# First routing stage: x laid out by partitions, tiles moved in pairs, router logits made with tokens on the partitions

## The chip, the cores and the metric

The kernel runs on one NeuronCore of a Trainium2 chip. The metric is the device time in microseconds (us) of one execution. An execution is made of one program that holds all stages of a two-layer network one behind the other; engines meet at a barrier between stages.

Engines are called PE (TensorE; PE for its matmuls, PEld for the loads of its stationary operand), DVE (VectorE), ACT (ScalarE), POOL (GpSimd) and SP (SyncE, which here only issues DMAs). A suffix q (SPq) means the engine's sequencer.

## What is computed

Activations are x, 2 x 2048 tokens by 512 features in fp32. The reference runs, in this order: a mixture-of-experts block, attention, the mixture block again, a gated feed-forward block, a second kind of attention, and the feed-forward block again. The change is in the first mixture block, whose routing part is:

```python
m = jnp.mean(x, axis=-1, keepdims=True); v = jnp.var(x, axis=-1, keepdims=True)
y = (x - m) / jnp.sqrt(v + 1e-5)                      # layer norm; y is the experts' input
var = jnp.mean(jnp.square(y), axis=-1, keepdims=True)
router_input = y * rsqrt(var + 1e-6) * 512 ** -0.5 * router_scale
logits = einsum('gsd,de->gse', router_input, router_logits)    # 8 experts
probs = softmax(logits); choices = top 2 of logits
# each token goes to its 2 experts, weighted by the renormalised probabilities
```

From the choices follows a plan: the pairs (token, expert) sorted by expert, cut into tiles of 128 slots, with the row of y that belongs into each slot.

## The kernel before

The 4096 tokens are 32 tiles of 128 tokens (NT = 32). In tile t, partition p holds token 128 t + p. `experts(0, x[0])` calls `routing_stage` and then `expert_stage`. The first routing (`given` is None) makes layer norm, the router's logits and the plan; the second routing gets its logits from `output_stage` (`given`) and only makes the plan, so that its tile loop does not exist.

The tile loop of the first routing, by engine:

- SP (L190 to L217) loads four tiles ahead (NX = 4, `load`, L193: 256 KB, 2 KB for each partition), then the router's weights `wl`, `rs` and the experts' scale `esc` on the same queue. For each tile it waits for y of that tile (L204), issues the load of the tile four later into the freed buffer, and the store of y to `yn` in DRAM (L207). After the loop it issues twelve loads of 512 KB with expert weights (L213).
- DVE (L345 on) first makes `wr`, the router's weights times the router's scale (L358), which waits for all three small loads. Then for each tile: `bn_stats` of the next tile (L362), reciprocal of the deviation (L378), `bn_aggr` of the next tile (L365), y itself (L384) and a copy of the variance (L369). y of tile t waits for the store that last used its buffer and for yT of tile t - 4.
- PE (L291 on): `turn` (L293) transposes a tile of y into PSUM with four matmuls against the identity (L297). `step` (L300) makes the logits of tile t with four fp32 matmuls, each of which the profile shows as two instructions (L304), and then turns tile t + 2. PE's order is thus turn 0, turn 1, logits 0, turn 2, logits 1, turn 3 and so on; its queue is served in this order. In the logits `wr` (128 x 8) is the stationary operand and the 128 columns of yT stream by, so the result has experts on the partitions: 8 x 128.
- ACT (L257 on): the deviation of the next tile (L261), yT from PSUM to SBUF (L267), and `keep` (L271), which copies the 8 x 128 logits of the tile before into `lgT` (L273).

Behind the loop PE turns the 32 pieces of `lgT` back to tokens on the partitions (L317 to L320, 32 transposes of 8 x 128), and DVE multiplies them with `rr`, the inverse of the root mean square (L408). DVE then picks the two best experts and makes the plan (L412 to L488). Meanwhile ACT and POOL prepare the weights of the first expert (L283 to L289, L253). `expert_stage` begins when all are done: its POOL gathers rows of `yn` by the plan (L536).

Two later places read or write what the change lays out anew: `projection_stage` loads tiles of x again (L860), and `output_stage` stores the y of the second mixture block to `yn` (L1514).

Of the kernel before, what the change touches and what calls it, by code (L numbers as in the profile page):

```python
# [15 lines left out]
ALU = mybir.AluOpType  # L16
# [3 lines left out]
P = 128  # L20
B, S, D = 2, 2048, 512
# [96 lines left out]
def routing_stage(nc, stage, const, x, scale, logits_w, expert_scale, w_experts, box, yn, plan, given=None):  # L118


    with ExitStack() as ctx:
        mem = Memory(nc, ctx, stage)
        NX = 4
        xb = mem.sb("xb", [P, NX, D])
        yb = mem.sb("yb", [P, NX, D])
# [40 lines left out]
        tr = mem.ps("tr", [P, 2, D])  # L166
        lg_ps = mem.ps("lg", [P, NT, E])
        pre_ps = mem.ps("pre", [P, E, NT])
# [3 lines left out]

        lgT_ps = [t[0:E].rearrange("e t f -> e (t f)")[:, 0:P] for t in (pre_ps, tot_ps)]
        tot_cols, count_ps = tot_ps[:, 0, 0:E // EH], tot_ps[:, 1, 0:E]

        x_in, y_st, raw_in = mem.sems("x_in", NX), mem.sems("y_st", NX), mem.sems("raw_in", WPIECES)
        whi_rdy, neg_rdy, wlo_in, next_in = mem.sem("whi_rdy"), mem.sem("neg_rdy"), mem.sems("wlo_in", 2), mem.sem("next_in")
        HOT = 8
        w_in, wr_rdy, iotas, ones_set, picked = (mem.sem(n) for n in ("w_in", "wr_rdy", "iotas", "ones_set", "picked"))
        bn_rdy, mv_rdy, sd_rdy, rstd_rdy, y_rdy, tr_rdy, yT_rdy, lgT_rdy, lgT_kept, lg_rdy = (  # L180
            mem.sem(n) for n in ("bn_rdy", "mv_rdy", "sd_rdy", "rstd_rdy", "y_rdy", "tr_rdy", "yT_rdy", "lgT_rdy", "lgT_kept", "lg_rdy"))
# [3 lines left out]
        block = ctx.enter_context(nc.Block())  # L185

        def piece(buf, n):
            return buf[:, n * WPIECE:(n + 1) * WPIECE]

        @block.sync  # L190
        def _(sp):
            def load(t, k):
                sp.dma_start(xb[:, k, :], x[bass.ds(t * P, P), :]).then_inc(x_in[k], 16)  # L193

            if not given:
                for t in range(NX):
                    load(t, t)
                    sp.sem_inc(y_st[t], 16)
                sp.dma_start(wl[:], logits_w).then_inc(w_in, 16)
                sp.dma_start(rs[:], scale).then_inc(w_in, 16)  # L200
            sp.dma_start(esc[:], expert_scale.partition_broadcast(P)).then_inc(w_in, 16)

            def step(t, k, i, last):
                sp.wait_ge(y_rdy, t + 1)  # L204
                if not last:
                    load(t + NX, k)
                sp.dma_start(yn[bass.ds(t * P, P), :], yb[:, k, :]).then_inc(y_st[k], 16)  # L207

            if not given:
                looped(sp, NT, NX, step)  # L210
            for n in range(2 * WPIECES):
                arrived = raw_in[n] if n < WPIECES else next_in
                sp.dma_start(piece(box["lo"], n).bitcast(F32), w_experts[n // WPIECES, :, n % WPIECES, :]).then_inc(arrived, 16)  # L213
            if not given:
                for k in range(NX):
                    sp.wait_ge(y_st[k], 16 * (NT // NX + 1))
            sp.wait_ge(next_in, 16 * WPIECES)  # L217

        @block.gpsimd
        def _(pool):  # L220
# [3 lines left out]
            pool.iota(iota_row[:], [[1, P]], base=0, channel_multiplier=0, allow_small_or_imprecise_dtypes=True).then_inc(iotas, 1)  # L224
            pool.iota(token[:], [[0, TOPK], [P, NT]], base=0, channel_multiplier=1, allow_small_or_imprecise_dtypes=True).then_inc(iotas, 1)
            pool.iota(number[:], [[0, 1]], base=0, channel_multiplier=1, allow_small_or_imprecise_dtypes=True).then_inc(iotas, 1)
# [30 lines left out]
        @block.scalar  # L257
        def _(act):
            def deviation(t, k):
                act.wait_ge(mv_rdy, t + 1)  # L260
                act.activation(sd[:, bass.ds(t, 1)], mv[:, k % 2, 1:2], ACT.Sqrt, bias=const["eps"][:]).then_inc(sd_rdy, 1)  # L261

            def step(t, k, i, last):
                if not (last and k == NX - 1):
                    deviation(t + 1, k + 1)
                act.wait_ge(tr_rdy, t + 1)
                act.activation(yT[:, k % 2, :], tr[:, k % 2, :], ACT.Copy).then_inc(yT_rdy, 1)  # L267
                if not (isinstance(t, int) and t == 0):
                    keep(t - 1, (k - 1) % 2)

            def keep(t, k):  # L271
                act.wait_ge(lgT_rdy, t + 1)
                act.activation(lgT[0:E, bass.ds(t, 1), :], lgT_ps[k].unsqueeze(1), ACT.Copy).then_inc(lgT_kept, 1)  # L273

            if not given:
                deviation(0, 0)
                looped(act, NT, NX, step, head=True)
                keep(NT - 1, (NT - 1) % 2)
                act.wait_ge(step_done, 3)
                act.activation(small["msd"][:], small["ms"][:], ACT.Sqrt).then_inc(msd_rdy, 1)  # L280
            act.wait_ge(gap_rdy, 1)
            act.activation(small["egap"][:], small["gap"][:], ACT.Exp).then_inc(egap_rdy, 1)
            for n in range(WPIECES):  # L283
                act.wait_ge(raw_in[n], 16)
                act.activation(piece(box["hi"], n), piece(box["lo"], n).bitcast(F32), ACT.Copy).then_inc(whi_rdy, 1)
                if n >= 2:
                    act.wait_ge(wlo_in[n % 2], 16 * (n // 2))
                act.wait_ge(whi_rdy, n + 1)
                act.activation(box["raw"][:, n % 2, :], piece(box["hi"], n).bitcast(F32), ACT.Copy, scale=-1.0).then_inc(neg_rdy, 1)  # L289

        @block.tensor  # L291
        def _(pe):
# [7 lines left out]
            def step(t, k, i, last):  # L300
                pe.wait_ge(yT_rdy, t + 5)
                pe.wait_ge(lgT_kept, t + 1)
                for c in range(DC):
                    ins = pe.matmul(lgT_ps[k % 2], wr[:, c, :], yT[:, k % 2, c * P:(c + 1) * P],  # L304
                                    start=(c == 0), stop=(c == DC - 1), skip_group_check=True)
                ins.then_inc(lgT_rdy, 1)
                if not (last and k >= NX - 2):
                    turn(t + 2, k + 2)

            if not given:  # L310
                pe.sem_inc(yT_rdy, 4)
                pe.sem_inc(lgT_kept, 2)
                pe.wait_ge(wr_rdy, DC)
                turn(0, 0)
                turn(1, 1)
                looped(pe, NT, NX, step)
                pe.wait_ge(lgT_kept, NT + 2)  # L317
                for t in range(NT):
                    ins = pe.transpose(lg_ps[:, t, :], lgT[0:E, t, :], const["ident"][0:E, 0:E])
                ins.then_inc(lg_rdy, 1)  # L320
            pe.wait_ge(both_rdy, 1)
# [24 lines left out]
        def _(dve):  # L346
            steps = [0]

            def then(ins):

                steps[0] += 1
                ins.then_inc(step_done, 1)
                dve.wait_ge(step_done, steps[0])
# [6 lines left out]
            def stats(t, k, i):  # L360
                dve.wait_ge(x_in[k], 16 * (i + 1))
                dve.bn_stats(bn[:, k % 2, :], xb[:, k, :]).then_inc(bn_rdy, 1)  # L362
# [8 lines left out]
            def step(t, k, i, last):  # L371
# [9 lines left out]
                dve.wait_ge(rstd_rdy, t + 1)  # L381
                dve.wait_ge(y_st[k], 16 * (i + 1))
                dve.wait_ge(yT_rdy, t + 1)
# [9 lines left out]
            else:  # L393
# [10 lines left out]
                then(dve.reciprocal(small["rr"][:], small["msd"][:]))  # L404
                dve.wait_ge(lg_rdy, 1)
                dve.wait_ge(iotas, 2)
                lg = wide["lg"]
                then(dve.tensor_tensor(lg[:], lg_ps[:], spread(small["rr"][:], E), ALU.mult))  # L408

# [412 lines left out]
def projection_stage(nc, stage, const, x, x_new, joined, q_w, k_w, v_w, q_parts, kst, v, spare):  # L822

    with ExitStack() as ctx:
# [33 lines left out]
        def _(sp):  # L858
            def load(t):
                sp.dma_start(xb[:, t % NX, :], x[bass.ds(t * P, P), :]).then_inc(x_in[t % NX], 16)  # L860

# [617 lines left out]
def output_stage(nc, stage, const, attn, w_hi, w_lo, x, x_new, scale, logits_w, yn, logits_out):  # L1479

    with ExitStack() as ctx:
# [26 lines left out]
        def _(sp):  # L1508
# [1021 lines left out]
def layout(np, i):  # L2530

    def chunked(w):
        return w.reshape(w.shape[0] // P, P, -1).transpose(1, 0, 2)
# [4 lines left out]
    def column(v):  # L2538
# [40 lines left out]
```

## Time and profile before

| | us |
|---|---|
| median of 3 runs | 4752.76 (4750.65 to 4758.85) |
| profiled execution, its own time | 4751.44 |
| span of the profiled execution | 4749.9 |
| first routing stage, to DVE's last instruction | 0 to 114.7 |
| expert stage 0, from PE's first instruction | 115.7 |

The page of the profile gives busy times of the engines over the whole span; for one stage the timeline, the windows and the waits are asked with a stretch in us from the start of the span. "PEclk" or "granted clock" is the share of TensorE's full clock: 1.00 is 2.4 GHz and 0.50 is 1.2 GHz. A timeline row is: start, duration, engine, line, operation, output<-inputs, shapes, count, and in brackets the idle time before it with what ended it. Several instructions that follow each other are one row with a count, and its duration is from the first start to the last end.

### The profile page before, as it was taken

To read this page: it belongs to the slowest core of one execution; us is meant where nothing else is said; L and a number is where in the kernel's file an instruction comes from. 1 tells how busy PE (TensorE), PEld (TensorE's weight loads), DVE (VectorE), ACT (ScalarE), POOL (GpSimd) and SP (SyncE) were. 2 spreads that over 40 slices of the span, in tenths; PEclk is the share of its full clock that TensorE was granted. 3 is DMA by queue.
4 is the path that set the end of the run, shared out by engine and by line. 5 is a ranking of instruction groups with operands and counts; after the bars stand their busy time and mean duration, and the time that the engine had idled before them with its cause. 6 is when DMAs were issued, how large, how long until landed. Compare 5 with 4: busy or idle time off the path is not lost. (4 is left out here: it accounts for less than half of the span.)

```text
span 4749.9 us, 81453 instructions
## 1 busy us (share of the span) xinstructions
PE 4566.0 (96%) x27934; PEld 3496.3 (74%) x27935; DVE 2873.2 (60%) x5253; ACT 2101.9 (44%) x4079; POOL 2252.9 (47%) x1724
## 2 busy tenths in 40 slices
PE   6999996899999999999999799999899999999999
PEld 4888885666666666666666688888788877778888
DVE  7222225789999999999984533323455548754444
ACT  4222224466676767676764322222333235433322
POOL 0545433278888888888882154643111007500000
PEclk8999998899999999999999799999899999999999
DMA  7232326757777777777765633433422112250110
GB/s 222 89 103 93 105 78 230 247 105 147 146 145 146 146 151 148 146 147 146 147 140 161 192 97 126 138 118 109 176 67 71 54 51 82 75 196 27 36 36 27
DMA packets 241401, 577.68 MB, mean 122 GB/s; under 512 B 30304, under 2 KB 84576, under 8 KB 216544
## 3 DMA queue, kind: packets, MB, share of 16 engines
q0 software_dynamic: 62064, 317.23, 29.7%
q1 hardware_dynamic: 178928, 255.47, 16.3%
q8 instruction: 198, 3.24, 0.3%
q14 instruction: 211, 1.73, 0.1%
HBM read 254.88 MB, written 121.63 MB: 79 GB/s over the span
## 5 line engine op out<-in xcount | busy, mean ns | idle before, releaser
L1410 POOL TENSOR_TENSOR attend_pairs<-attend_pt 128x1024 f32<-128x1024 f32 x512 | 1258.5, 2476 | 197.8 <-ACT attend_pt L1375 197.6
L1423 DVE TENSOR_REDUCE attend_mx<-attend_am_ps 128x1 f32<-128x512 f32 x2048 | 1251.4, 678 | 126.4 <-PE attend_am_ps L1283 123.0
L1375 ACT ACTIVATE attend_pt<-attend_sc_ps 128x512 f32<-128x512 f32 x2048 | 1040.2, 617 | 284.5 <-PE attend_sc_ps L1271 284.4
L1283 PE MATMUL attend_am_ps<-attention_kst,attend_qst 96*128 96x512 f32 x2048 | 859.9, 425 | 10.8 <-DMA attend_qst<-q_parts 10.7
L1271 PE MATMUL attend_sc_ps<-attend_qst,attention_kst 98*128 98x512 f32 x2048 | 816.9, 400 | 1.5 <-ACT attend_pt L1375 1.3
L1283 PEld LDWEIGHTS attend_am_ps<-attention_kst,attend_qst 96*128 96x128 f32 x2048 | 393.2, 192 | 241.4 <-DVE attend_mx L1423 123.1
L1775 PE MATMUL ffn_gu_ps<-ffn_y_hi,ffn_w 128*128 128x512 f32 (+1 forms) x1584 | 567.0, 367 | 3.1 <-DVE ffn_y_lo L1905 3.0
L1775 PE MATMUL ffn_gu_ps<-ffn_y_lo,ffn_w 128*128 128x512 f32 (+1 forms) x1584 | 566.3, 367 | 0.0
L768 DVE TENSOR_TENSOR expert_ac<-expert_gu_ps,expert_gl 128x512 f32<-128x512 f32 x142 | 98.2, 691 | 748.1 <-ACT expert_gl L715 748.1
L1297 PE MATMUL attend_pv_ps<-attend_pt,attention_v 128*32 128x256 f32 x8192 | 493.6, 381 | 0.0
L1271 PEld LDWEIGHTS attend_sc_ps<-attend_qst,attention_kst 98*128 98x128 f32 x2048 | 389.8, 191 | 87.7 <-ACT attend_pt L1375 11.7
L1297 PEld LDWEIGHTS attend_pv_ps<-attend_pt,attention_v 128*32 128x32 f32 x8192 | 246.2, 110 | 211.8 <-ACT attend_pt L1375 46.4
L1847 ACT ACTIVATE ffn_sg<-ffn_gu_ps,ffn_gs 128x512 f32<-128x512 f32 (+1 forms) x198 | 127.4, 644 | 568.4 <-PE ffn_gu_ps L1775 568.2
L715 ACT ACTIVATE expert_gl<-expert_gu_ps 128x512 f32<-128x512 f32 x142 | 85.0, 599 | 628.9 <-PE expert_gu_ps L645 628.9
L645 PE MATMUL expert_gu_ps<-weights_hi,expert_x_hi 128*128 x1088 | 342.5, 396 | 4.6 <-issue 1.8
L1775 PEld LDWEIGHTS ffn_gu_ps<-ffn_y_hi,ffn_w 128*128 128x128 f32 x1584 | 300.6, 190 | 52.5 <-DVE ffn_y_lo L1905 3.6
L1775 PEld LDWEIGHTS ffn_gu_ps<-ffn_y_lo,ffn_w 128*128 128x128 f32 x1584 | 300.7, 190 | 48.1
L645 PE MATMUL expert_gu_ps<-weights_lo,expert_x_hi 128*128 x1088 | 335.9, 390 | 0.0
L645 PE MATMUL expert_gu_ps<-weights_hi,expert_x_lo 128*128 x1088 | 335.4, 389 | 0.0
L1915 DVE SCALAR_TENSOR_TENSOR ffn_hf<-ffn_gu_ps,ffn_us,ffn_sg 128x512 f32<-128x512 f32 (+1 forms) x198 | 136.9, 691 | 318.9 <-PE ffn_gu_ps L1775 311.1
L1791 PE MATMUL ffn_dn_ps<-ffn_w,ffn_h_hi 128*128 128x512 f32 x704 | 276.6, 393 | 0.0
L1791 PE MATMUL ffn_dn_ps<-ffn_w,ffn_h_lo 128*128 128x512 f32 x704 | 274.2, 390 | 0.0
(350 smaller groups left out, 7461.6 us busy)
## 6 DMA issues: line engine op xcount, KB each, us to landing
attend_pairs<-attend_pairs POOLq DMA_DIRECT2D x189, 1024.0 KB, 7.4
weights_raw<-experts_dram POOLq DMA_DIRECT2D x76, 512.0 KB, 4.1
ys<-expert_ob SPq DMA_DIRECT2D x142, 256.0 KB, 2.0
attend_qst<-q_parts SPq DMA_DIRECT2D x192, 128.0 KB, 3.9
ffn_xb<-x SPq DMA_DIRECT2D x64, 256.0 KB, 2.9
keyvalue_xb<-x SPq DMA_DIRECT2D x64, 256.0 KB, 2.8
weights_lo<-experts_dram SPq DMA_DIRECT2D x24, 512.0 KB, 8.9
ffn_w<-ffn_kept SPq DMA_DIRECT2D x22, 512.0 KB, 9.2
```

The source lines that it names most:

```text
L645: ins = pe.matmul(gu[:, q, :], a, w[:, bass.ds(off + (c * WPIECE + q * H), H)], start=(c == 0 and n == 0), stop=(c == DC - 1 and n == 2))
L768: dve.tensor_tensor(ac[:, k, :], gu[:, 1, :], gl[:, k, :], ALU.mult).then_inc(ac_rdy, 1)
L1271: pe.matmul(sc[:, s % SBANKS, :], kst[0:KROWS + 2, o:o + P], qst[0:KROWS + 2, n % 2, hh:hh + 4, :], start=True, stop=True).then_inc(s_rdy, 1)
L1283: pe.matmul(am[:, bank, :], qst[0:KROWS, n % 2, h * HALF + hd, :], kst[0:KROWS, o:o + 4 * P], start=True, stop=True).then_inc(am_rdy, 1)
L1297: ins = pe.matmul(pv[HD * j:HD * (j + 1), 0, :], v[:, (n // QT) * QT + kt, :], pt[:, u % RING, 2 * P * j:2 * P * (j + 1)], start=(kt == 0) ...
L1375: act.activation(pt[:, u % RING, g * 4 * P:(g + 1) * 4 * P], sc[:, s % SBANKS, :], ACT.Exp, scale=HD ** -0.5).then_inc(p_rdy, 1)
L1410: pool.tensor_tensor(pairs[:, slot(half, j), :], pt[:, 2 * p % RING, :], pt[:, (2 * p + 1) % RING, :], ALU.add).then_inc(pair_rdy, 1)
L1423: dve.tensor_reduce(mx[:, hh, block:block + 1], am[:, am_slot["max", a] % MBANKS, :], AX.X, ALU.max).then_inc(mx_rdy, 1)
L1775: ins = pe.matmul(gu[:, k, q, 0:width], a, b, start=(c == 0 and n == 0), stop=(c == DC - 1 and n == 1))
L1791: ins = pe.matmul(dn[:, j % 2, :], a, b, start=(m == 0 and n == 0), stop=(m == IC - 1 and n == 1))
L1847: act.activation(sg[:, k, 0:n], gu[:, k, 0, 0:n], ACT.Silu, scale=gs[:, m:m + 1]).then_inc(sg_rdy, 1)
L1915: dve.scalar_tensor_tensor(hf[:, k, 0:n], gu[:, k, 1, 0:n], us[:, m:m + 1], sg[:, k, 0:n], ALU.mult, ALU.mult).then_inc(h_rdy, 1)
```

## The change

In the first routing x comes from the host laid out as 128 partitions x 32 tiles x 512 (`chunked`), so that two neighbouring tiles are 4 KB in a row for each partition, 64 KB from one partition to the next. Tiles are loaded and y is stored in pairs of 512 KB, with eight tiles (four pairs) in flight; the eight load buffers lie in the space of `lgT`, which no longer holds logits. `yn` gets the same order: token (tile t, partition p) is row 32 p + t; `token` in the plan follows, and so do the store in `output_stage` and the load in `projection_stage`, which stay single tiles. In the logits the operands swap: yT (128 x 128) is the stationary operand and the 8 columns of `wr` stream by, so that the result is 128 tokens x 8 and `keep` copies it straight to `lg`. The 32 transposes behind the loop go. The loop is unrolled eight times instead of four.

```diff
-        NX = 4
-        xb = mem.sb("xb", [P, NX, D])
+        NX = 8
...
+        xb = lgT[:].rearrange("p (n a) b -> p n (a b)", n=NX)
...
-        lgT_ps = [t[0:E].rearrange("e t f -> e (t f)")[:, 0:P] for t in (pre_ps, tot_ps)]
+        lg_ps = [t[:, 0:1, 0:E] for t in (pre_ps, tot_ps)]
...
-            def load(t, k):
-                sp.dma_start(xb[:, k, :], x[bass.ds(t * P, P), :]).then_inc(x_in[k], 16)
+            def load(pair, k):
+                sp.dma_start(xb[:, 2 * k:2 * k + 2, :], x[:, bass.ds(pair * 2, 2), :]).then_inc(x_in[k], 16)
...
-            def step(t, k, i, last):
-                sp.wait_ge(y_rdy, t + 1)
+            def step(pair, k, i, last):
+                sp.wait_ge(y_rdy, pair * 2 + 2)
                 if not last:
-                    load(t + NX, k)
-                sp.dma_start(yn[bass.ds(t * P, P), :], yb[:, k, :]).then_inc(y_st[k], 16)
+                    load(pair + NX // 2, k)
+                sp.dma_start(y_rows[:, bass.ds(pair * 2, 2), :], yb[:, 2 * k:2 * k + 2, :]).then_inc(y_st[k], 16)
...
-            pool.iota(token[:], [[0, TOPK], [P, NT]], base=0, channel_multiplier=1, ...)
+            pool.iota(token[:], [[0, TOPK], [1, NT]], base=0, channel_multiplier=NT, ...)
...
             def keep(t, k):
-                act.wait_ge(lgT_rdy, t + 1)
-                act.activation(lgT[0:E, bass.ds(t, 1), :], lgT_ps[k].unsqueeze(1), ACT.Copy).then_inc(lgT_kept, 1)
+                act.wait_ge(lg_rdy, t + 1)
+                act.activation(wide["lg"][:, bass.ds(t, 1), :], lg_ps[k], ACT.Copy).then_inc(lg_kept, 1)
...
                 for c in range(DC):
-                    ins = pe.matmul(lgT_ps[k % 2], wr[:, c, :], yT[:, k % 2, c * P:(c + 1) * P],
+                    ins = pe.matmul(lg_ps[k % 2], yT[:, k % 2, c * P:(c + 1) * P], wr[:, c, :],
                                     start=(c == 0), stop=(c == DC - 1), skip_group_check=True)
...
                 looped(pe, NT, NX, step)
-                pe.wait_ge(lgT_kept, NT + 2)
-                for t in range(NT):
-                    ins = pe.transpose(lg_ps[:, t, :], lgT[0:E, t, :], const["ident"][0:E, 0:E])
-                ins.then_inc(lg_rdy, 1)
...
-                dve.wait_ge(lg_rdy, 1)
+                dve.wait_ge(lg_kept, NT + 2)
                 lg = wide["lg"]
-                then(dve.tensor_tensor(lg[:], lg_ps[:], spread(small["rr"][:], E), ALU.mult))
+                then(dve.tensor_tensor(lg[:], lg[:], spread(small["rr"][:], E), ALU.mult))
...
# projection_stage
-                sp.dma_start(xb[:, t % NX, :], x[bass.ds(t * P, P), :]).then_inc(x_in[t % NX], 16)
+                sp.dma_start(xb[:, t % NX, :], x[:, t, :]).then_inc(x_in[t % NX], 16)
...
# output_stage
-                sp.dma_start(yn[t * P:(t + 1) * P, :], yb[:, t % NX, :]).then_inc(y_st[t % NX], 16)
+                sp.dma_start(yn.rearrange("(p t) d -> p t d", t=NT)[:, t, :], yb[:, t % NX, :]).then_inc(y_st[t % NX], 16)
...
-        "x": i["L0_attn_x"].reshape(T, D),
+        "x": chunked(i["L0_attn_x"].reshape(T, D)),
```

## Rows read from the trace of the kernel before

**Rows 1.** The page, busy us with share of the span and instructions.

```profile
PE 4566.0 (96%) x27934; PEld 3496.3 (74%) x27935; DVE 2873.2 (60%) x5253; ACT 2101.9 (44%) x4079; POOL 2252.9 (47%) x1724
```

**Rows 2.** Windows: stretch, length, busy us of five engines, PEclk, DMA share, GB/s.

```profile
4.00:8.00 4.00, 0.00 (x0) 0.00 (x0) 0.00 (x0) 0.46 (x1) 2.31 (x34) 1.00 0.88 269
20.00:40.00 20.00, 17.03 (x128) 11.18 (x128) 15.68 (x54) 11.51 (x33) 0.00 (x0) 1.00 0.89 274
40.00:60.00 20.00, 16.89 (x128) 10.98 (x125) 15.45 (x54) 11.85 (x33) 0.00 (x0) 1.00 0.91 275
78.00:82.00 4.00, 0.00 (x0) 0.00 (x0) 3.73 (x10) 0.00 (x0) 0.00 (x0) 0.53 1.03 421
```

**Rows 3.** Waits of DVE, 0 to 110 us: total us, times, longest.

```profile
DVE route_wr L358 <- DMA route_esc<-expert_scale_dram: 9.0, 1, 9.0
DVE route_bn L362 <- DMA route_xb<-x_dram: 6.3, 11, 0.9
```

**Rows 4.** Timeline of DVE, y of tiles 0, 29 and 31.

```profile
11.87 0.55 DVE L384 TENSOR_SCALAR route_yb<-route_xb,route_mv,route_rstd 128x512 f32<-128x512 f32 x1
...
67.13 0.55 DVE L384 TENSOR_SCALAR route_yb<-route_xb,route_mv,route_rstd 128x512 f32<-128x512 f32 x1
...
70.19 0.55 DVE L384 TENSOR_SCALAR route_yb<-route_xb,route_mv,route_rstd 128x512 f32<-128x512 f32 x1
```

**Rows 5.** Timeline of PE, first tiles of the loop.

```profile
12.52 1.09 PE L297 MATMUL route_tr_ps<-all_ident,route_yb 128*128 128x128 f32 x4 [12.52 <-DVE route_yb L384]
14.01 1.12 PE L297 MATMUL route_tr_ps<-all_ident,route_yb 128*128 128x128 f32 x4 [0.40 <-DVE route_yb L384]
15.06 1.88 PE L304 MATMUL route_pre_ps<-route_yT,route_wr 128*8 128x128 f32 x8
16.86 0.66 PE L297 MATMUL route_tr_ps<-all_ident,route_yb 128*128 128x128 f32 x4
17.45 1.04 PE L304 MATMUL route_tot_ps<-route_yT,route_wr 128*8 128x128 f32 x8
```

**Rows 6.** Timeline of PE, the last tiles of the output stage.

```profile
2662.36 0.95 PE L1644 MATMUL output_lg_ps<-output_wr,output_yT 128*128 128x8 f32 x8
...
2664.49 1.06 PE L1644 MATMUL output_lg_ps<-output_wr,output_yT 128*128 128x8 f32 x8 [0.69 <-ACT output_yT L1544]
2665.41 1.80 PE L1636 MATMUL output_tr_ps<-all_ident,output_yb 128*128 128x128 f32 x8
2667.05 3.58 PE L1644 MATMUL output_lg_ps<-output_wr,output_yT 128*128 128x8 f32 x16
```

**Rows 7.** Windows in the plan and in the output stage, columns as in rows 2.

```profile
96.00:114.00 18.00, 14.99 (x68) 14.07 (x66) 17.90 (x30) 4.69 (x5) 2.58 (x3) 0.50 0.59 117
2650.00:2662.00 12.00, 12.00 (x73) 10.45 (x72) 7.03 (x17) 3.95 (x8) 0.00 (x0) 1.00 0.39 146
2666.00:2670.00 4.00, 4.00 (x20) 3.77 (x19) 0.52 (x2) 1.31 (x3) 0.00 (x0) 0.50 0.18 67
```

**Rows 8.** Timeline of the routing's loop end, from the last logits on.

```profile
72.42 1.04 PE L304 MATMUL route_tot_ps<-route_yT,route_wr 128*8 128x128 f32 x8
...
73.49 0.27 ACT L273 ACTIVATE route_lgT<-route_tot_ps 8x128 f32<-8x128 f32 x1 [0.61 <-PE route_tot_ps L304]
...
73.81 2.14 PE L319 MATMUL route_lg_ps<-all_ident,route_lgT 8*128 8x8 f32 x32 [0.36 <-ACT route_lgT L273]
...
73.98 0.35 DVE L404 RECIPROCAL route_rr<-route_msd 128x32 f32<-128x32 f32 x1 [2.70 <-ACT route_msd L280]
76.04 0.42 DVE L408 TENSOR_TENSOR route_lg<-route_lg_ps,route_rr 128x256 f32<-128x256 f32 x1 [1.71 <-PE route_lg_ps L319]
```

**Rows 9.** Timeline: POOL's last weight add and DVE's last instruction of the stage.

```profile
103.07 0.86 POOL L253 DMA_DIRECT2D weights_lo<-weights_raw  x1 [1.76 <-ACT weights_raw L289]
...
114.48 0.23 DVE L488 CAST weights_rows<-route_rows_ps 128x72 uint32<-128x72 f32 x1 [0.33 <-PE route_rows_ps L342]
```

**Rows 10.** Windows, inside the projection stage, columns as in rows 2.

```profile
820.00:880.00 60.00, 58.31 (x288) 46.76 (x287) 57.21 (x122) 34.38 (x68) 24.57 (x26) 1.00 1.02 369
```

More of the change, by code:

```diff
@@ L166, in routing_stage @@
         tr = mem.ps("tr", [P, 2, D])
-        lg_ps = mem.ps("lg", [P, NT, E])
         pre_ps = mem.ps("pre", [P, E, NT])
@@ L171, in routing_stage @@
         tab_ps = mem.ps("tab", [1, 5, SLOT_TILES])
-        lgT_ps = [t[0:E].rearrange("e t f -> e (t f)")[:, 0:P] for t in (pre_ps, tot_ps)]
+        lg_ps = [t[:, 0:1, 0:E] for t in (pre_ps, tot_ps)]
         tot_cols, count_ps = tot_ps[:, 0, 0:E // EH], tot_ps[:, 1, 0:E]
-        x_in, y_st, raw_in = mem.sems("x_in", NX), mem.sems("y_st", NX), mem.sems("raw_in", WPIECES)
+        x_in, y_st, raw_in = mem.sems("x_in", NX // 2), mem.sems("y_st", NX // 2), mem.sems("raw_in", WPIECES)
         whi_rdy, neg_rdy, wlo_in, next_in = mem.sem("whi_rdy"), mem.sem("neg_rdy"), mem.sems("wlo_in", 2), mem.sem("next_in")
@@ L179, in routing_stage @@
         w_in, wr_rdy, iotas, ones_set, picked = (mem.sem(n) for n in ("w_in", "wr_rdy", "iotas", "ones_set", "picked"))
-        bn_rdy, mv_rdy, sd_rdy, rstd_rdy, y_rdy, tr_rdy, yT_rdy, lgT_rdy, lgT_kept, lg_rdy = (
-            mem.sem(n) for n in ("bn_rdy", "mv_rdy", "sd_rdy", "rstd_rdy", "y_rdy", "tr_rdy", "yT_rdy", "lgT_rdy", "lgT_kept", "lg_rdy"))
+        bn_rdy, mv_rdy, sd_rdy, rstd_rdy, y_rdy, tr_rdy, yT_rdy, lg_rdy, lg_kept = (
+            mem.sem(n) for n in ("bn_rdy", "mv_rdy", "sd_rdy", "rstd_rdy", "y_rdy", "tr_rdy", "yT_rdy", "lg_rdy", "lg_kept"))
         step_done, msd_rdy, gap_rdy, egap_rdy, both_rdy, summed, totals_rdy, ranked, tile_rdy, token_rdy, row_rdy, rows_rdy, tab_rdy, turned = (
@@ L185, in routing_stage @@
         block = ctx.enter_context(nc.Block())
+        y_rows = yn.rearrange("(p t) d -> p t d", t=NT)
         def piece(buf, n):
@@ L191, in _ @@
         def _(sp):
-            def load(t, k):
-                sp.dma_start(xb[:, k, :], x[bass.ds(t * P, P), :]).then_inc(x_in[k], 16)
+            def load(pair, k):
+                sp.dma_start(xb[:, 2 * k:2 * k + 2, :], x[:, bass.ds(pair * 2, 2), :]).then_inc(x_in[k], 16)
             if not given:
-                for t in range(NX):
-                    load(t, t)
-                    sp.sem_inc(y_st[t], 16)
+                for pair in range(NX // 2):
+                    load(pair, pair)
+                    sp.sem_inc(y_st[pair], 16)
                 sp.dma_start(wl[:], logits_w).then_inc(w_in, 16)
@@ L201, in _ @@
             sp.dma_start(esc[:], expert_scale.partition_broadcast(P)).then_inc(w_in, 16)
-            def step(t, k, i, last):
-                sp.wait_ge(y_rdy, t + 1)
+            def step(pair, k, i, last):
+                sp.wait_ge(y_rdy, pair * 2 + 2)
                 if not last:
-                    load(t + NX, k)
-                sp.dma_start(yn[bass.ds(t * P, P), :], yb[:, k, :]).then_inc(y_st[k], 16)
+                    load(pair + NX // 2, k)
+                sp.dma_start(y_rows[:, bass.ds(pair * 2, 2), :], yb[:, 2 * k:2 * k + 2, :]).then_inc(y_st[k], 16)
             if not given:
-                looped(sp, NT, NX, step)
+                looped(sp, NT // 2, NX // 2, step)
             for n in range(2 * WPIECES):
@@ L214, in _ @@
             if not given:
-                for k in range(NX):
+                for k in range(NX // 2):
                     sp.wait_ge(y_st[k], 16 * (NT // NX + 1))
@@ L224, in _ @@
             pool.iota(iota_row[:], [[1, P]], base=0, channel_multiplier=0, allow_small_or_imprecise_dtypes=True).then_inc(iotas, 1)
-            pool.iota(token[:], [[0, TOPK], [P, NT]], base=0, channel_multiplier=1, allow_small_or_imprecise_dtypes=True).then_inc(iotas, 1)
+            pool.iota(token[:], [[0, TOPK], [1, NT]], base=0, channel_multiplier=NT, allow_small_or_imprecise_dtypes=True).then_inc(iotas, 1)
             pool.iota(number[:], [[0, 1]], base=0, channel_multiplier=1, allow_small_or_imprecise_dtypes=True).then_inc(iotas, 1)
@@ L301, in step @@
                 pe.wait_ge(yT_rdy, t + 5)
-                pe.wait_ge(lgT_kept, t + 1)
+                pe.wait_ge(lg_kept, t + 1)
                 for c in range(DC):
-                    ins = pe.matmul(lgT_ps[k % 2], wr[:, c, :], yT[:, k % 2, c * P:(c + 1) * P],
+                    ins = pe.matmul(lg_ps[k % 2], yT[:, k % 2, c * P:(c + 1) * P], wr[:, c, :],
                                     start=(c == 0), stop=(c == DC - 1), skip_group_check=True)
-                ins.then_inc(lgT_rdy, 1)
+                ins.then_inc(lg_rdy, 1)
                 if not (last and k >= NX - 2):
@@ L311, in _ @@
                 pe.sem_inc(yT_rdy, 4)
-                pe.sem_inc(lgT_kept, 2)
+                pe.sem_inc(lg_kept, 2)
                 pe.wait_ge(wr_rdy, DC)
@@ L360, in stats @@
             def stats(t, k, i):
-                dve.wait_ge(x_in[k], 16 * (i + 1))
+                dve.wait_ge(x_in[k // 2], 16 * (i + 1))
                 dve.bn_stats(bn[:, k % 2, :], xb[:, k, :]).then_inc(bn_rdy, 1)
@@ L381, in step @@
                 dve.wait_ge(rstd_rdy, t + 1)
-                dve.wait_ge(y_st[k], 16 * (i + 1))
+                if k % 2 == 0:
+                    dve.wait_ge(y_st[k // 2], 16 * (i + 1))
                 dve.wait_ge(yT_rdy, t + 1)
```

## Prediction

> **What bounds the kernel now.** I read the page first: PE is busy for 96% of the span, but that is an average over stages, and the change touches one of 115 us [rows 1]. So I ask that stage: windows, waits, timeline. In the tile loop no engine is full: in 20 us PE is busy for 17.0, DVE for 15.7, and the DMA engines are 0.89 to 0.91 busy at 274 GB/s [rows 2]. DVE's waits say what is late: 6.3 us for tiles of x, and 9.0 us for the small loads ahead of the loop [rows 3]. y of tile 0 starts at 11.87 and of tile 31 at 70.19, 1.88 us a tile; undisturbed tiles (29 to 31) take 3.06 / 2 = 1.53 us [rows 4]. So the loop is bound by DMA on top of a DVE that is nearly as slow, and PE, with 0.59 us of transposes and about 1 us of logits a tile [rows 5], is close behind. All three matter: whichever gets slower sets the end.
>
> After the loop a serial chain of DVE ends the stage at 114.7; ACT's and POOL's weight work issues its last add at 103.07 [rows 9] and has 7 us to spare after some 4.5 of landing, so it follows any shift of the loop unseen. Each microsecond of the loop is one of the kernel, since the stages behind start at a barrier.
>
> **The start.** The first four loads carry 2.1 MB instead of 1.05 MB, and the small loads wait behind them. Between 4 and 8 us 1.08 MB came at 269 GB/s; loads with 4 KB for each partition (expert weights) run at 421 GB/s [rows 2]. At that rate 2.1 MB take 5.0 us instead of 4: +1.0 us for `wr` and so for y 0 (12.9). Bounds: 0, if the small loads slip through, and +3.8, if 4 KB gain nothing (1.05 MB at 275). I take 1.0, because the weight loads have the same packet size.
>
> **DMA in the loop.** A tile moves 524 KB in and out: 1.9 us at 275 GB/s, 1.25 us at 421 [rows 2]. Loads at the new size leave the path; what pairs add in waiting (y leaves after every second tile, the first load after two) is hidden by six more tiles in flight. By this alone DVE would set about 1.55 us a tile.
>
> **PE in the loop, the step that decides.** Per tile PE keeps four transposes and eight logits instructions, but each logits instruction now loads 128 x 128 and streams 8 columns, where it loaded 128 x 8 and streamed 128. The output stage does just this operation (L1644): eight in 0.95 us at full clock [rows 6]. At full clock nothing is lost.
>
> Will the clock be at 2.4 GHz? The loop before starts slow: four transposes take 1.09 us at 12.52, 0.66 at 16.86 [rows 5]. So PE ran at the lower level until some 3 us of transposes and of logits that stream 128 columns were behind it (the windows print 1.00 there, since no change was recorded before; the durations tell). In the output stage PE has 1.00 while 512-column products fill it. When these end, at 2662.4, and only transposes and new-form logits are left, PE goes on in 2664.49 and 2665.41 and the clock falls in the middle of it; from 2666 to 2670 PE is busy for 4.00 of 4.00 us with transposes and these logits, the same mix as the new loop, and the clock stays at 0.50 [rows 6, 7]. The plan agrees: 64 matmuls with a full weight load and 72 columns keep PE busy for 15 of 18 us, at 0.50 throughout [rows 7]. I conclude that in this mix being busy does not bring the clock. The new loop begins at 1.2 GHz, as the old one did, and from its third group has nothing but this mix: it stays at 1.2 GHz to its end.
>
> The Trainium skill ("TensorE: Matmul & The Clock Gate", "HAM oscillation — how this bites in real kernels") speaks against that: it asks only that PE has no idle gaps. PE has none in the new loop, so by the page the clock is full, and the forecast turns into rival 1. The trace disagrees with the page in 2666 to 2670 [rows 7].
>
> **Price at 1.2 GHz.** In the cold start of the old loop the turn group took 15.06 - 14.01 = 1.05 us, the logits group 16.86 - 15.06 = 1.80 us, each to the next group's start, with nothing but PE late [rows 5]. The new logits are no cheaper: 16 in a row took 3.58 us at 0.50 [rows 6], against 1.88 for eight of the old form [rows 5], so eight more cost 1.70, 0.213 each, plus the change of group. From the start of logits 0 to the end of logits 31 there are 32 logits groups and 30 turns: 32 x 1.80 + 30 x 1.05 = 89.1 us. Lower end: 12 instructions at 0.213 without gaps, 32 x 1.70 + 30 x 0.85 = 79.9 us. I take 87, near the upper one, which contains this loop's own group changes. PE then needs 2.8 us a tile, and DVE (1.55) and DMA (1.25 to 1.9) are covered, as is ACT with its three short operations; y of tile t waits for yT of t - 4, so DVE only runs ahead and idles.
>
> Logits 0 start at 15.06 + 1.0 = 16.1, the last end at 103.1.
>
> **The end of the loop.** Before, the last logits end at 73.46, ACT copies to 73.76, `rr` is ready at 74.33, and the 32 transposes hold DVE's L408 until 76.04 [rows 8]. Without them L408 waits for `rr`: 0.9 us after the last logits, which is 1.7 saved. What is late next is ACT (copy, then root). L408 comes at 104.0: 104.0 - 76.04 = +28.0 us. The weight loads start about four tiles before PE's end, earlier against the plan than before; they had slack already, so nothing is gained. The plan runs at 0.50 in both kernels.
>
> **The other edits.** `token` is a constant: nothing. The buffers in `lgT` are free when the plan writes there. Rows gathered for the experts are 2 KB as before: 0, bound by rival 2. The store of y in `output_stage` lies beside a PE that is busy for 12.0 of 12 us [rows 7]: 0. The load in `projection_stage` keeps 2 KB pieces but strides by 64 KB, and there the DMA engines are full at 369 GB/s [rows 10]: 0 if stride costs nothing, rival 2 otherwise.
>
> **Sum.** 4751.4 (profiled execution's own time) + 28.0 = 4779.4 us, its span about 4778. The median of the runs is 1.3 us above the profiled one: 4780.8, so 4781.
>
> **Rivals.**
> 1. *The clock is granted; faster.* It decides in the first groups: if PE's first transposes lift the clock and the mix holds it, y 31 starts at 12.9 + 31 x 1.55 = 61.0; L408 before came 3.3 + 0.9 = 4.2 us after y 31 without the transposes [rows 4, 8], so at 65.2, -10.9 us: 4742 on the median's scale. For it: DMA was the bound, and the new rate is seen. Against it: rows 6 and 7, and only eight transposes stand ahead of the first new logits, where the old loop went straight on with 128-column streams.
> 2. *The stride of 64 KB costs.* 8.4 MB of x are loaded in the DMA-bound projection; at half of 369 GB/s they take 23 us more. On top of the forecast: 4804. For it: that stage has no DMA slack [rows 10]. Against it: expert weights come in strided by 24 KB at the full 421 [rows 2], and gathered rows of 2 KB keep the 369 up beside them. The Trainium skill ("DMA: Bandwidth & Descriptors", "Latency and other measured facts") puts a loss at much larger pitches, 2 MiB and up; no row here has either.
> 3. *The clock is granted for part of the loop*, as where a group of transposes falls well: half the loop at each level gives (28 - 11) / 2 = +8.5, 4761.
>
> **Chances.** Forecast 0.80, rival 1 0.11, rival 2 0.04, rival 3 0.05. The forecast's own range is 4772 to 4787: the lower PE price takes 7 off, the upper adds 2, the start adds up to 2.8, and the rest is spread of runs. With some of rival 3 and of a dearer start the range is 4765 to 4789; rival 1, most of rival 2 and half of rival 3 stay out. About 0.2% (9.5 us) is what a measurement can tell from no change. Slower: forecast, rival 2 and half of rival 3, 0.86. Faster: most of rival 1, 0.09. Same: 0.05.
>
> **What would show it.** Right: in the loop granted clock 0.50, four transposes at about 1.1 us, eight logits near 1.8, PE without idle time, DVE waiting for PE or ACT and no longer for x, y about 2.8 apart, L408 near 104, L319 gone. The start is right if y 0 comes at 12.9. Wrong: windows of 20:60 with clock 1.00 and y about 1.55 apart (rival 1), or a projection stage longer than before by more than 2 us (rival 2). Also wrong in size if the eight logits at 0.50 take 1.7 with no gap, or more than 2.

## The result and the profile after

The changed kernel takes 4771.7 us (median of 6 runs, 4768.31 to 4773.98); the kernel before took 4751.03 us beside it (6 runs, 4749.99 to 4758.85). The ratio is 1.0036, 95% interval 1.0026 to 1.0046: slower, by 12 to 22 us by the interval, with the medians 20.7 apart. Of the executions below, one of 9181 us (moves_only) and one of 6575 us (pad_loop) are in no ratio, but one of 4779 us (pad_loop) and one of 4803 us (pad_small_first) are. The forecast was 4781 (4765 to 4789): direction and mechanism held, the size was 9 us too large.

The page after, busy us with share of the span, and the span of the profiled execution, +20.0 us [rows 1]:

```profile
span 4769.9 us, 81196 instructions
PE 4591.3 (96%) x27902; PEld 3539.7 (74%) x27903; DVE 2872.6 (60%) x5253; ACT 2100.1 (44%) x4079; POOL 2255.3 (47%) x1724
```

PE has 25 us more work in 32 fewer instructions. The windows of the changed stage, columns as in rows 2, say where (between the first and the second line the tile loop begins at 14.55):

```profile
4.00:8.00 4.00, 0.00 (x0) 0.00 (x0) 0.00 (x0) 0.46 (x1) 2.33 (x34) 1.00 0.94 302
20.00:40.00 20.00, 20.00 (x101) 20.00 (x99) 11.59 (x43) 8.06 (x25) 0.00 (x0) 1.00 0.78 233
40.00:60.00 20.00, 20.00 (x99) 20.00 (x100) 11.74 (x41) 8.93 (x25) 0.00 (x0) 1.00 0.74 210
```

PE and its weight loads fill the whole of the loop, where no engine was full before [rows 2], and DMA has become idle for a quarter of it. The 1.00 under PEclk is no measurement here either: no change of the clock was recorded before the expert stage. The durations tell, on PE's timeline from the first tile:

```profile
15.20 1.09 PE L297 MATMUL route_tr_ps<-all_ident,route_yb 128*128 128x128 f32 x4 [15.20 <-DVE route_yb L381]
16.69 1.12 PE L297 MATMUL route_tr_ps<-all_ident,route_yb 128*128 128x128 f32 x4 [0.41 <-DVE route_yb L381]
17.60 1.72 PE L304 MATMUL route_pre_ps<-route_wr,route_yT 128*128 128x8 f32 x8
19.17 1.09 PE L297 MATMUL route_tr_ps<-all_ident,route_yb 128*128 128x128 f32 x4
20.05 1.71 PE L304 MATMUL route_tot_ps<-route_wr,route_yT 128*128 128x8 f32 x8
21.62 1.09 PE L297 MATMUL route_tr_ps<-all_ident,route_yb 128*128 128x128 f32 x4
22.51 1.72 PE L304 MATMUL route_pre_ps<-route_wr,route_yT 128*128 128x8 f32 x8
```

Four transposes stay at 1.09 us, the duration that the kernel before had only in its first two groups [rows 5]: the loop runs at 1.2 GHz. A tile takes 22.51 - 20.05 = 2.46 us, of which logits 1.57 and transposes 0.89, start to start. The loads of the stationary operand (PEld) show why hardly anything is lost between groups:

```profile
19.84 1.83 PEld L304 LDWEIGHTS route_tot_ps<-route_wr,route_yT 128*128 128x128 f32 x8
21.41 0.90 PEld L297 LDWEIGHTS route_tr_ps<-all_ident,route_yb 128*128 128x128 f32 x4
22.30 1.83 PEld L304 LDWEIGHTS route_pre_ps<-route_wr,route_yT 128*128 128x128 f32 x8
```

The first load of the transposes begins at 21.41, before the last logits load ends (21.67). DVE's timeline gives the start and the end of the loop, and its waits what it was late for:

```profile
11.71 0.63 DVE L354 TENSOR_SCALAR route_wr<-route_wl,route_rs 128x8 f32<-128x8 f32 x4 [11.71 <-DMA route_esc<-expert_scale_dram]
...
14.55 0.55 DVE L381 TENSOR_SCALAR route_yb<-route_lgT,route_mv,route_rstd 128x512 f32<-128x512 f32 x1
...
88.64 0.55 DVE L381 TENSOR_SCALAR route_yb<-route_lgT,route_mv,route_rstd 128x512 f32<-128x512 f32 x1
...
95.44 0.42 DVE L405 TENSOR_TENSOR route_lg<-route_lg,route_rr 128x256 f32<-128x256 f32 x1
...
133.89 0.23 DVE L485 CAST weights_rows<-route_rows_ps 128x72 uint32<-128x72 f32 x1 [0.33 <-PE route_rows_ps L338]
```

```profile
DVE route_rstd L374 <- ACT route_sd L261: 30.4, 29, 1.6
DVE route_wr L354 <- DMA route_esc<-expert_scale_dram: 11.7, 1, 11.7
DVE route_rr L401 <- ACT route_msd L280: 5.3, 1, 5.3
```

No wait for x is left [rows 3]; DVE waits for ACT's deviation, which stands in ACT's order behind `keep`, and `keep` behind PE's logits. y 0 is 2.68 us later than before [rows 4], the multiplication by `rr` 19.40 later, and the stage's last instruction 133.89 - 114.48 = 19.41 [rows 8, 9]. So the whole shift of this stage arises before that multiplication, and 2.68 of it at the start. The other stages differ by less than 1 us each, except the first expert stage, 640.1 us from its first PE instruction to the first load of the next stage, against 638.7.

### The profile page after: what moved, and what is told of

Its sections match the earlier page's. It is cut to its first block and busy times, and to the rows that moved or that the text cites. A ratio compares the mean times of both kernels' runs of the same rounds, so it can differ in the third digit from the quotient of the medians.

```text
span 4769.9 us, 81196 instructions
## 1 busy us (share of the span) xinstructions
PE 4591.3 (96%) x27902; PEld 3539.7 (74%) x27903; DVE 2872.6 (60%) x5253; ACT 2100.1 (44%) x4079; POOL 2255.3 (47%) x1724
## 3 DMA queue, kind: packets, MB, share of 16 engines
q14 instruction: 211, 1.73, 0.1%
```

## The experiments

The first table is read off all kernels' timelines: start of y 0, start of the multiplication by `rr` ("product"), and the time between them, which is the loop and its end without the start. The times are medians; before had 4751.0 beside the changed kernel and 4755.1 to 4755.7 beside the others, so that the ratios compare them better than the times. A ratio's interval is 4 to 10 us to either side, and it weighs all executions, not the middle one; what happens inside the stage is read from "between".

| kernel | y 0 | product | between | time | ratio to before |
|---|---|---|---|---|---|
| before | 11.87 | 76.04 | 64.17 | | |
| after | 14.55 | 95.44 | 80.89 | 4771.7 | 1.0036 [1.0026, 1.0046] |
| logits_only | 12.93 | 93.82 | 80.89 | 4768.4 | 1.0028 [1.0018, 1.0039] |
| small_first | 11.11 | 92.00 | 80.89 | 4768.2 | 1.0026 [1.0017, 1.0035] |
| warm_start | 14.47 | 93.67 | 79.20 | 4771.0 | 1.0031 [1.0019, 1.0043] |
| moves_only | 14.28 | 72.15 | 57.87 | 4750.1 | 0.9988 [0.9979, 0.9997] |
| depth_only | 14.87 | 72.43 | 57.56 | 4749.9 | 0.9986 [0.9977, 0.9995] |
| moves_small_first | 10.99 | 68.90 | 57.91 | 4747.4 | 0.9984 [0.9975, 0.9992] |
| pad_loop | 14.57 | 73.99 | 59.42 | 4750.4 | 0.9995 [0.9982, 1.0008] |
| pad1_small_first | 11.09 | 65.44 | 54.35 | 4745.4 | 0.9994 [0.9980, 1.0008] |
| pad_small_first | 11.12 | 70.61 | 59.49 | 4746.2 | 0.9989 [0.9969, 1.0010] |

**The swap of the operands alone (logits_only).** The kernel before, with the new logits and without the 32 transposes; loads, layout and depth as before.

```diff
-                    ins = pe.matmul(lgT_ps[k % 2], wr[:, c, :], yT[:, k % 2, c * P:(c + 1) * P],
+                    ins = pe.matmul(lg_ps[k % 2], yT[:, k % 2, c * P:(c + 1) * P], wr[:, c, :],
```

> Before, with the logits' operands swapped and nothing else: single tiles of 256 KB, four in flight, x and yn in the old order, no transposes behind the loop. Theory A (PE stays at 1.2 GHz because only transposes and logits with 8 streamed columns are left, and the loop is bound by PE): a tile takes 2.45 us as in the changed kernel, y of tile 0 stays at 11.9 us, the multiply with rr comes 80.9 us later at 92.8 instead of 76.0, so 16.7 us slower than before: 4768. Theory B (the time went into the layout, the pairs and the later start, the logits only look slow because they wait): no slower than before, rather 1.7 us faster for the transposes that go: 4749 to 4751.

Measured 4768.4. Its y 0 came at 12.93 although no load differs from before (11.87), so the landing of the small loads moves by a microsecond between such kernels; counted from y 0, the swap costs 80.89 - 64.17 = 16.72 us, to the hundredth what the whole change shows. The time is 0.28% above before (0.18 to 0.39), 9 to 19 us. The window:

```profile
20.00:40.00 20.00, 20.00 (x99) 20.00 (x100) 11.38 (x40) 8.54 (x25) 0.00 (x0) 1.00 0.74 218
```

All of the loop's loss is the swap; the rest of the 19.40 is the start.

**Layout, pairs and depth alone (moves_only).** The changed kernel with the old logits and the 32 transposes; the load buffers lie in a half of the weights' space that is free in this stage.

```diff
-                    ins = pe.matmul(lg_ps[k % 2], yT[:, k % 2, c * P:(c + 1) * P], wr[:, c, :],
+                    ins = pe.matmul(lgT_ps[k % 2], wr[:, c, :], yT[:, k % 2, c * P:(c + 1) * P],
```

> The changed kernel with the old logits (wr stationary, 128 columns streamed, transposes behind the loop); layout by partitions, pairs and eight tiles in flight stay, the load buffers lie in the unused half of the experts' weight buffer. Theory A: granted clock 2.4 GHz from about the third tile, DVE no longer waits for x and sets about 1.55 us a tile; y of tile 0 at 14.5 us, y of tile 31 at 62.6, the multiply with rr at 68.5 instead of 76.0: 7.5 us faster than before, 4743.5. Theory B: the layout and the pairs cost the 20 us, so this kernel is near 4771 too. A smaller part: if the 64 KB stride costs in the projection stage, that stage is longer than 179.3 us.

Measured 4750.1, faster than before by 0.12% (0.03 to 0.21). The waits for x are gone and the rate is up, but y comes every 1.68 us and not every 1.55. The window and DVE's largest wait in the loop, then ACT's timeline:

```profile
20.00:40.00 20.00, 19.38 (x144) 12.59 (x143) 16.64 (x60) 12.60 (x36) 0.00 (x0) 1.00 0.93 285
40.00:60.00 20.00, 19.59 (x150) 13.01 (x150) 17.47 (x62) 13.07 (x38) 0.00 (x0) 1.00 0.98 325
```

```profile
DVE route_rstd L381 <- ACT route_sd L264: 5.9, 13, 1.5
```

```profile
40.51 0.60 ACT L270 ACTIVATE route_yT<-route_tr_ps 128x512 f32<-128x512 f32 x1 [0.32 <-PE route_tr_ps L300]
41.57 0.27 ACT L276 ACTIVATE route_lgT<-route_tot_ps 8x128 f32 x1 [0.46 <-PE route_tot_ps L307]
41.75 0.29 ACT L264 ACTIVATE route_sd<-route_mv,all_eps 128x1 f32 x1
42.06 0.60 ACT L270 ACTIVATE route_yT<-route_tr_ps 128x512 f32<-128x512 f32 x1
```

At 41.75 the next tile's deviation starts right behind the copy of the logits, which waited for PE; PE is busy for 19.4 to 19.6 of 20 us. So y, transposes, logits, copy, deviation and the next y form a chain in ACT's order. PE itself is nearly as slow: where it waits for nothing, its transposes start 0.59 us (39.81 to 40.40) before the logits and these 0.97 us before the next transposes, 1.56 us a tile. The chain is read from the trace, not tested: no kernel here changes ACT's order.

**Depth alone (depth_only).** The kernel before with NX = 8: eight single-tile loads in flight, 2 KB for each partition. The same constant gives y eight buffers and unrolls the loop eight times, as in the changed kernel; layout and logits are the old ones.

```diff
-        NX = 4
-        xb = mem.sb("xb", [P, NX, D])
+        NX = 8
+        xb = box["hi"][:, WPIECES * WPIECE:WPIECES * WPIECE + NX * D].bitcast(F32).rearrange("p (n d) -> p n d", n=NX)
```

> Before, with eight tiles in flight instead of four and the loop unrolled eight times; single loads and stores of 256 KB with 2 KB for each partition, old layout, old logits. It parts depth from packet size. Theory G (before, the loop lacked rate: 275 GB/s is what 2 KB pieces give in both directions): depth helps little, 1.80 to 1.88 us a tile, and the start is later, because 2.1 MB at 270 GB/s stand ahead of the small loads (wr at 12.5 to 13 instead of 9.0): 2 to 4 us slower than before. Theory H (it lacked depth, the waits for x were latency): 1.65 to 1.70 us a tile as in moves_only, the multiply with rr 2 to 4 us earlier than before.

Measured 4749.9, with 1.67 us a tile and no waits for x:

```profile
20.00:40.00 20.00, 19.39 (x144) 12.82 (x144) 16.44 (x60) 12.82 (x37) 0.00 (x0) 1.00 0.94 299
40.00:60.00 20.00, 19.57 (x148) 13.08 (x148) 17.63 (x62) 13.22 (x38) 0.00 (x0) 1.00 0.95 323
```

2 KB pieces move 299 to 323 GB/s with eight in flight, against 274 with four [rows 2]. The depth removed the DMA bound; the layout and the pairs add nothing to it that the loop shows.

**The clock lifted before the loop (warm_start).** The changed kernel with 42 dummy matmuls (84 instructions of 128 columns) ahead of the first transposes, while DVE still makes the first y. They leave nothing in the result.

```diff
+                warm(pe, const, tr[:, 1, 0:P], 42)
```

> The changed kernel with 42 dummy matmuls (128 x 128 against 128 columns, result unused) on PE before the first tile, while PE waits for x anyway. Theory A (the mix of transposes and 8-column logits neither brings the full clock nor keeps it): PE starts the loop at 2.4 GHz and falls back within the first few tiles; at most 2 to 4 us are won: 4768 to 4771. Theory C (the mix can't lift the clock but keeps it, once it is there): all tiles at 2.4 GHz, PE needs about 1.4 to 1.5 us a tile, DVE sets 1.55, the loop ends some 28 us earlier: 4743.

Measured 4771.0. PE's timeline, from the last 19 of the 84 instructions on:

```profile
13.76 2.29 PE L93 MATMUL route_tr_ps<-all_ones,all_ident 128*128 128x128 f32 x19
15.88 1.39 PE L297 MATMUL route_tr_ps<-all_ident,route_yb 128*128 128x128 f32 x8
17.25 1.05 PE L304 MATMUL route_pre_ps<-route_wr,route_yT 128*128 128x8 f32 x8
18.29 0.66 PE L297 MATMUL route_tr_ps<-all_ident,route_yb 128*128 128x128 f32 x4
18.78 0.96 PE L304 MATMUL route_tot_ps<-route_wr,route_yT 128*128 128x8 f32 x8
19.83 1.11 PE L297 MATMUL route_tr_ps<-all_ident,route_yb 128*128 128x128 f32 x4
20.73 1.71 PE L304 MATMUL route_pre_ps<-route_wr,route_yT 128*128 128x8 f32 x8
```

```profile
12.00:20.00 8.00, 7.77 (x66) 7.16 (x65) 7.09 (x26) 3.15 (x10) 0.00 (x0) 0.99 0.27 56
20.00:40.00 20.00, 20.00 (x99) 20.00 (x100) 11.87 (x41) 8.01 (x25) 0.00 (x0) 0.50 0.79 243
40.00:60.00 20.00, 20.00 (x100) 20.00 (x99) 11.36 (x40) 8.77 (x25) 0.00 (x0) 0.50 0.75 211
```

The loop starts at 2.4 GHz (transposes 0.66, logits 0.96), falls at about 19.8 and stays at 0.50, with PE busy for 20.00 of 20 us. The clock was recorded here, and the durations are those of the changed kernel. So its loop does not stay slow because it starts slow: this mix gives the full clock away when it has it. PE was busy for 2.49 of the 2.58 us from the first new logits (17.25) to the transposes at 19.83.

**The mix made heavier (pad_loop).** The same with two dummy matmuls (four instructions of 128 columns) for each tile behind the transposes: 128 instructions more.

```diff
+                warm(pe, const, pad_ps[:], 2)
```

> As warm_start, and in each tile two more dummy matmuls (four instructions of 128 x 128 against 128 streamed columns) ahead of the logits. It adds work to PE in each of the 32 tiles. Theory A: the clock stays at 2.4 GHz; PE needs 16 instructions at 0.11 us and gaps, 1.8 to 1.9 us a tile instead of 2.45, so the loop ends 18 to 20 us earlier than in the changed kernel: 4752 to 4754. Theory D (the loop is bound by the loads of the stationary operand whatever the clock): each tile gets 0.43 to 0.85 us longer, 14 to 27 us slower than the changed kernel: 4786 or more.

Measured 4750.4, and the product comes at 73.99, 21.4 us earlier than in the changed kernel and 19.7 earlier than in warm_start, from which it differs by these 128 instructions alone, though PE has more to do:

```profile
20.00:40.00 20.00, 19.88 (x181) 19.60 (x182) 15.84 (x57) 10.97 (x35) 0.00 (x0) 1.00 1.00 303
40.00:60.00 20.00, 19.79 (x180) 19.54 (x180) 15.92 (x56) 11.21 (x34) 0.00 (x0) 1.00 0.97 288
```

```profile
20.19 0.63 PE L298 MATMUL route_tr_ps<-all_ident,route_yb 128*128 128x128 f32 x4
20.66 0.61 PE L93 MATMUL route_pad_ps<-all_ones,all_ident 128*128 128x128 f32 x4
21.10 0.96 PE L306 MATMUL route_pre_ps<-route_wr,route_yT 128*128 128x8 f32 x8
21.92 0.63 PE L298 MATMUL route_tr_ps<-all_ident,route_yb 128*128 128x128 f32 x4
```

A tile takes PE 21.92 - 20.19 = 1.73 us, 0.44 of it the dummies. That the loss could lie in the loads of the stationary operand, and not in the clock, is refuted: the same logits instructions are there, at 0.96 us for eight. Nor was it the short gap in warm_start: here PE stood for 1.22 us of the 3.65 ahead of the first logits (14.00 to 17.65) and kept the clock. Whether the padding brings the clock without the 84 instructions ahead of the loop was not tried.

**The small loads first (small_first).** The changed kernel with the loads of `wl`, `rs` and `esc` ahead of x on SP's queue.

```diff
-                for pair in range(NX // 2):
-                    load(pair, pair)
-                    sp.sem_inc(y_st[pair], 16)
...
+            if not given:
+                for pair in range(NX // 2):
+                    load(pair, pair)
+                    sp.sem_inc(y_st[pair], 16)
```

> The changed kernel with the three small loads issued ahead of the four loads of pairs instead of behind them. Theory E (the router's weights wait behind 2.1 MB, and since the loop is bound by PE at 1.2 GHz the start passes to the end in full): wr is ready before x, y of tile 0 starts 2.3 us after its pair lands, near 10 to 10.5 us instead of 14.55, the loop's period stays 2.45, the multiply with rr comes at 91 to 91.5 instead of 95.4: some 4 us faster than the changed kernel, 4767. Theory F (the start is hidden by the tiles in flight): the end of the loop stays at 95.4, 4771.

Measured 4768.2. DVE's timeline:

```profile
6.83 0.63 DVE L355 TENSOR_SCALAR route_wr<-route_wl,route_rs 128x8 f32<-128x8 f32 x4 [6.83 <-DMA route_esc<-expert_scale_dram]
8.80 0.69 DVE L359 BATCH_NORM_STATS2 route_bn<-route_lgT 128x6 f32<-128x512 f32 x1 [1.35 <-DMA route_lgT<-x_dram]
...
11.11 0.55 DVE L382 TENSOR_SCALAR route_yb<-route_lgT,route_mv,route_rstd 128x512 f32<-128x512 f32 x1
```

`wr` comes 4.88 us earlier, but then DVE waits 1.35 us for the first pair of x: y 0 gains 3.44 us, and the product gains the same 3.44. What the start loses or gains passes to the end in full.

**Combinations.** moves_only with the small loads first (moves_small_first):

> As moves_only (old logits, new layout, pairs, eight in flight), with the small loads first. The loop of moves_only took 1.68 us a tile and was bound by the engines, not by the loads. So by theory E y of tile 0 comes 4 us earlier, at 10 to 10.5 us, and the multiply with rr at 68 instead of 72.15: 4 us less than moves_only, 8 us less than before, 4743 to 4746. By theory F, or if the loop then waits for x, it keeps 4748 to 4750.

Measured 4747.4, ratio 0.9984 [0.9975, 0.9992]: the surest gain of all kernels here. Its product is 7.14 us earlier than before.

The new logits with the small loads first and half the padding, one dummy matmul a tile (pad1_small_first):

> The changed kernel with the small loads first, 26 dummy matmuls ahead of the loop and one dummy matmul (two instructions) per tile, half of pad_loop's. Theory A has no figure for where the clock tips; if half the padding still keeps 2.4 GHz, a tile takes 1.6 to 1.7 us (1.76 in pad_loop), y of tile 0 at 10.5, the multiply at 66: 10 us less than before, 4742. If it doesn't, the clock falls to 1.2 GHz within a few tiles, a tile takes 2.45 + 0.43 = 2.9 us and the kernel is near 4780.

The profiled execution has the shortest loop of all (54.35 between, granted clock 1.00), but the 12 times fall into two groups, seven of 4738 to 4746 us and five of 4761 to 4768. The mean granted clock of each execution parts them too: 0.974 to 0.976 in the seven, 0.969 or 0.970 in the five. So I tried the full padding with the small loads first (pad_small_first):

> The changed kernel with the small loads ahead of x, 26 dummy matmuls of 128 columns ahead of the loop and two for each tile (four instructions). The dummies leave nothing in the result. pad1_small_first, with half the padding, had two groups of times, 4738 to 4746 and 4761 to 4768. Theory: in the second group the clock fell within the loop; with two dummies for each tile it does not, as in pad_loop. Then there is one group, near pad_loop's 4750.4 less the 3.4 that small_first gained: 4747, and the span near 4743. The product lg x rr comes at 73.99 - 3.4 = 70.6 or earlier, granted clock 1.00 from 20 to 60. Rival: the two groups have another cause than the padding; then times near 4765 are seen here too, in about 4 of 10 executions.

Eleven of the 12 times lie between 4742.8 and 4750.3 (mean clock 0.973 to 0.976), one at 4803 (0.962); none near 4765. The product came at 70.61, as expected. So half the padding holds the clock only in some executions. That the five lose it in this loop is inferred: 0.005 less over 4765 us is 48 us more at half clock, which fits a loop that loses it partway, but none of the five was profiled. The full padding is not safe either: besides the 4803, one execution of pad_loop took 4779 us at 0.968. Against moves_small_first this version is no better within the intervals.

## Why the prediction came out as it did

**Right: the mix does not bring the clock.** The forecast rested on 4 us of the output stage and on the plan [rows 6, 7]. warm_start shows it from 20 us to the loop's end, and logits_only that nothing else is needed. Rivals 1 and 3 are out for the changed kernel. The rule of the Trainium skill ("TensorE: Matmul & The Clock Gate", "HAM oscillation — how this bites in real kernels"), that PE loses the clock by idle gaps, does not account for this: in warm_start PE was busy for 20.00 of 20.00 us at granted clock 0.50. In the output stage PE had stood for 0.69 us ahead of the fall [rows 6], so that those rows alone did not rule a gap out; in warm_start it stood for 0.09.

**Right: what it replaces.** The waits for x are gone, DVE waits for ACT behind PE, the 32 transposes are gone (the product came 0.8 us behind the last logits, predicted 0.9), and POOL's weight adds followed the loop unseen: the stage shifted by 19.41 and the product by 19.40.

**Wrong in size: PE's price in the loop.** I took 87 us from the start of logits 0 to the end of logits 31, between 79.9 and 89.1. Measured were 17.60 to 94.62, 77.0 us: 32 x 1.57 + 30 x 0.89 = 76.9. The step that failed is "The new logits are no cheaper": the logits group was priced at the old form's 1.80 [rows 5] and is 1.57. The 1.70 worked out from the output stage [rows 6] is too dear as well, so that the lower end, 12 instructions at 0.213, was none. And the turn group at 1.05 is 0.89 in the new loop, where the next group's first load overlaps the last of this one. The term is 10.0 us too large.

**Wrong in size: the start.** +1.0 predicted, +2.68 measured, within the bounds of 0 to 3.8. The 4 KB pieces did bring nearly the rate of the weight loads, but not from the first byte:

```profile
4.00:6.00 2.00, 0.00 (x0) 0.00 (x0) 0.00 (x0) 0.46 (x1) 1.93 (x33) 1.00 0.86 209
7.00:10.00 3.00, 0.00 (x0) 0.00 (x0) 0.00 (x0) 0.00 (x0) 0.00 (x0) 1.00 1.02 411
```

The step that failed is "At that rate 2.1 MB take 5.0 us instead of 4". It priced all 2.1 MB at 421 GB/s, while the 4 us for the first megabyte hold its slow beginning (164 GB/s from 4 to 5 us in the kernel before). The second megabyte alone takes 1.05 MB / 411 GB/s = 2.6 us, and that is what came on top. How much of it is chance is open: logits_only, with the loads of before, had its small loads 1.06 us later (10.09 against 9.03), while the four kernels with pairs of x ahead of the small loads had them at 11.44 to 11.72. Logits 0 began at 17.60 and not at 16.1. The product came 104.0 - 95.44 = 8.56 us before its forecast: 10.0 for PE's price less 1.5 for the start, and 0.1 at the end.

**Wrong in cause: what lifted the DMA bound.** I put the higher rate down to packets of 4 KB. depth_only has 2 KB and the same loop to 0.3 us. The sum was not touched, since PE covered the transfers, but rival 1's price was: at full clock the loop runs at 1.61 us a tile (pad1_small_first) to 1.68 (moves_only) and not at 1.55, which the trace of moves_only puts down to ACT's order.

**Rival 2, the stride of 64 KB.** The projection stage took 179.6 us against 179.3, and inside it the rate is the same [rows 10]:

```profile
840.00:900.00 60.00, 58.30 (x290) 46.76 (x289) 57.26 (x119) 34.45 (x68) 24.63 (x26) 1.00 1.02 369
```

The stride costs nothing that can be seen. The Trainium skill ("DMA: Bandwidth & Descriptors", "Latency and other measured facts") is in line with that: its copies lose clearly from a pitch of 2 MiB up, and the smallest pitch that it lists, 512 KiB, is far above the 64 KB here.

**Missing from the sum: the first expert stage.** It took 1.4 us more than before, and that is a dip of the clock. The windows and PE's rows of the stage's first large products, the changed kernel and then the kernel before:

```profile
142.80:146.30 3.50, 3.49 (x9) 2.79 (x10) 0.37 (x1) 0.95 (x1) 2.70 (x6) 0.52 0.66 198
143.82 1.05 PE L642 MATMUL expert_gu_ps<-weights_lo,expert_x_hi 128*128 x2
...
123.40:126.90 3.50, 3.50 (x15) 2.93 (x16) 0.29 (x1) 0.87 (x1) 2.67 (x6) 1.00 0.64 192
123.96 0.63 PE L645 MATMUL expert_gu_ps<-weights_lo,expert_x_hi 128*128 x2
```

The first twelve of these products take 4.40 us from start to start (142.81 to 147.21) against 2.87 (123.39 to 126.26), 1.53 more. The five kernels whose trace has this dip (changed, moves_only, depth_only, small_first, moves_small_first) take 639.9 to 640.2 us for the stage, the six without it (before and logits_only among them) 638.3 to 639.5. It is not the swap, for moves_only has it and logits_only does not, and not the deeper loads by themselves, for pad_loop has them and no dip. Why the clock falls there in some kernels is open.

## What to carry to other kernels

Of two operand orders with the same number of matmuls, the one that streams 8 columns over a fresh 128 x 128 operand is equal at full clock (0.96 against 1.04 us for eight), but in a loop of little else (here four transposes to eight such instructions) it can cost the full clock itself: look in the trace for a stretch that already runs the planned mix, and read its granted clock and not its busy share. When a loop waits for loads, first deepen the loads in flight before its layout is changed; and put small operands that gate the loop ahead of the large ones on their queue.

## What was not expected of the hardware

- More work on PE made the loop faster: 128 added instructions of 128 columns took 19.7 us off it (pad_loop against warm_start), by holding 2.4 GHz.
- A busy PE at full clock gives the clock up: in warm_start it fell some 2.6 us after the first logits of the new form, 0.09 us of them idle, and it was still at 0.50 when the loop ended.
- At 1.2 GHz, fp32 instructions that each load 128 x 128 follow each other about every 0.2 us (1.57 for eight, 0.89 for four), whether 8 or 128 columns stream; a change of group costs about 0.1 us. At 2.4 GHz in pad_loop it was 0.82 for eight.
- 2 KB pieces moved 323 GB/s with eight loads in flight, 275 with four, in the same loop and the same window (40 to 60 us).
